# Second attention: scores in plain float32 from one tile of queries and one of key blocks, in place of three passes on high and low parts

## The reference

```
Qp = query @ Wq + bq
K = _l2norm(key @ Wk + bk)
V = value @ Wv + bv
Q = _l2norm(Qp)
... split in 16 heads of 16
scores = einsum('bhqd,bhkd->bhqk', Q, K) * SCALE
attn = softmax(scores)
out = einsum('bhqk,bhkd->bhqd', attn, V)
x = out @ Wo + bo + Qp          # then a layer norm
```

## Time and profile before

| What | Value |
|---|---|
| median of 3 runs | 942.38 us (939.27 to 947.75) |
| the profiled execution | 947.8 us, span 946.0 us |
| mean granted TensorE clock over the span | 0.951 |
| PE busy over the span | 867.4 us (92%) |
| DVE, ACT, POOL busy | 723.1, 527.6, 366.6 us |
| scores of attention 1 (L2112) | 240 matmuls, 50.9 us busy |
| values of attention 1 (L2128) | 640 matmul records, 84.4 us busy |
| query split on DVE (L2330) | 16 operations, 0.657 to 0.692 us each |
| key blocks on POOL (L2549) | 16 operations, 1.37 to 1.40 us each |

### The profile page before, as it was taken

One profiled execution on the slowest core, in us unless ns is written; L12 is line 12 of the kernel. 1 busy time (PEld: TensorE's weight loads), 2 busy tenths in 40 slices (PEclk: granted clock), 3 DMA queues, 4 the chain that ended last, 5 costly groups with the idle time before them and its releaser, 6 DMA issues. The chain is left out here.

```text
span 946.0 us, 18647 instructions
## 1 busy us (share of the span) xinstructions
PE 867.4 (92%) x5904; PEld 793.7 (84%) x5904; DVE 723.1 (76%) x1821; ACT 527.6 (56%) x1454; POOL 366.6 (39%) x412
## 2 busy tenths in 40 slices
PE   5899999999999999999979999996899999999435
PEld 5889999999999988898978999995688888888324
DVE  6788788878878978878656677784525889877888
ACT  4776567656747645546244444443435566664277
POOL 3234333424333426756521211413544757431230
PEclk9999999999999999999999999997768999999758
DMA  9999970000100013434125434434111111000003
GB/s 287 311 336 326 333 229 0 0 0 0 34 0 1 1 34 96 127 108 140 62 85 146 122 110 148 141 124 122 35 50 35 51 40 46 23 1 2 0 22 156
DMA packets 51771, 91.89 MB, mean 97 GB/s; under 512 B 5381, under 2 KB 26298, under 8 KB 51697
## 3 DMA queue, kind: packets, MB, share of 16 engines
q1 hardware_dynamic: 45105, 72.87, 24.0%
q0 software_dynamic: 6592, 18.07, 6.1%
HBM read 34.56 MB, written 56.36 MB: 96 GB/s over the span
## 5 line engine op out<-in xcount | busy, mean ns | idle before, releaser
L535 POOL TENSOR_TENSOR prob<-prob,row_inv 128x462 f32<-128x462 f32 (+1 forms) x96 | 83.8, 875 | 178.8 <-DVE row_inv L711 178.8
L898 PE MATMUL acc<-u,probT 128*128 128x256 f32 (+1 forms) x960 | 134.2, 289 | 1.0 <-DVE u L723 1.0
L595 ACT ACTIVATE prob<-score,neg_max 128x77 f32<-128x77 f32 x512 | 121.2, 353 | 13.3 <-DVE neg_max L705 12.9
L851 PE MATMUL score<-m,xnT 128*128 128x462 f32 (+1 forms) x576 | 122.7, 350 | 0.0
L898 PEld LDWEIGHTS acc<-u,probT 128*128 128x128 f32 (+1 forms) x960 | 119.5, 189 | 1.9 <-DVE u L723 1.4
L851 PEld LDWEIGHTS score<-m,xnT 128*128 128x128 f32 x576 | 96.3, 188 | 5.8
L2128 PEld LDWEIGHTS acc<-vz,prob 128*128 128x128 f32 (+1 forms) x640 | 82.4, 203 | 13.0 <-issue 11.2
L1231 PE MATMUL py<-w1T,hidT 128*128 x426 | 93.0, 354 | 0.0
L585 ACT ACTIVATE probT<-tr 128x512 fp32r<-128x512 f32 (+1 forms) x96 | 52.0, 545 | 66.2 <-PE tr L837 65.8
L1676 POOL DMA_INDIRECT dispatched<-xn,slots x64 | 69.5, 1085 | 43.8 <-DVEq L1460 26.5
L2128 PE MATMUL acc<-vz,prob 128*128 128x34 f32 (+2 forms) x640 | 84.4, 287 | 0.0
(11 more groups left out here) (381 smaller groups left out, 2100.5 us busy)
## 6 DMA issues: line engine op xcount, KB each, us to landing
dispatched<-zeros SPq DMA_DIRECT2D x1, 33664.0 KB, 109.2
xn<-dispatched SPq DMA_DIRECT2D x71, 128.0 KB, 2.0
dispatched<-hid SPq DMA_DIRECT2D x71, 128.0 KB, 1.8
out<-x_res SPq DMA_DIRECT2D x7, 512.0 KB, 2.6
x_res<-in_x SPq DMA_DIRECT2D x1, 3072.0 KB, 15.2
consts<-in_L_ffn_W SPq DMA_DIRECT2D x8, 384.0 KB, 3.5
consts<-in_L_ffn_Ws SPq DMA_DIRECT2D x3, 384.0 KB, 3.6
x_res<-in_x SPq DMA_DIRECT2D x2, 512.0 KB, 10.2
```

The source lines that it names most:

```text
L535: gp.tensor_tensor(pr, pr, row_inv[t % 2][:, heads(k)].unsqueeze(2).to_broadcast([P, BANK_HEADS[k], KEYS]), ALU.mult).then_inc(prob_ready, 1)
L595: last = act.activation(prob[t % 2][:, h * KEYS:(h + 1) * KEYS], score_of(t, k)[:, n * KEYS:(n + 1) * KEYS], ACT.Exp, bias=neg_max[t % 2][ ...
L851: last = pe.matmul(score_of(t, k)[:, 0:BANK_HEADS[k] * KEYS], xnT[blk][i][:, dc, j * P:(j + 1) * P], m[w][:, dc, cols(k)], start=(n == 0 a ...
L898: last = pe.matmul(acc[t % 2][:, 0:D], probT[t % 2][i][0:rows, c, :], u[k][0:rows, c, :], start=(c == 0 and q == 0), stop=(c == KCH - 1 an ...
```

## The change

The high and low tiles go away, for queries and for keys. ACT's copy out of the turned bank becomes the only one, in float32, and its semaphore takes the place of the low part's. POOL builds one `kbd`, in one operation where there were two. The scores of a chunk are one float32 matmul call, started and closed in itself, and the calls of a pair stand one behind the other. Nothing else in any engine's order is moved.

```diff
-    kept = g["consts"][:, KEPT_AT:KEPT_AT + DC * CK].bitcast(F32R).rearrange("p (c k) -> p c k", k=CK)
-    g["k1T"] = [kept, right("k1T_lo", [P, DC, CK], F32R)[:, :, :]]
+    g["k1T"] = g["consts"][:, KEPT_AT:KEPT_AT + DC * CK].rearrange("p (c k) -> p c k", k=CK)
...
-                act.activation(g["k1T"][0][:, f, :], side[:, 0:CK], ACT.Copy).then_inc(s["kT_hi"], 1)
+                act.activation(g["k1T"][:, f, :], side[:, 0:CK], ACT.Copy).then_inc(s["kT_out"], 1)
...
-            if i - 2 in TURN_AT:
-                f = TURN_AT.index(i - 2)
-                dve.wait_ge(s["kT_hi"], f + 1)
-                dve.tensor_tensor(g["k1T"][1][:, f, :], side[:, 0:CK], f32(g["k1T"][0][:, f, :]), ALU.subtract).then_inc(s["kT_lo"], 1)
...
-        kbd = [sb(f"kbd1_{i}", [P, DC, HH, KEYS], F32R) for i in range(2)]
+        kbd = sb("kbd3", [P, DC, HH, KEYS], F32)
...
-        qT = [[sb(f"qT{s}_{i}", [P, DC, TB], F32R) for i in range(2)] for s in range(2)]
+        qT = [sb(f"qT{s}", [P, DC, TB], F32) for s in range(2)]
...
-                pe.wait_ge(s["qT_lo"], DC * n + f + 1)
+                pe.wait_ge(s["qT_out"], DC * n + f + 1)
...
-            for q, (i, k) in enumerate(HI_LO_PASSES):
-                keys = kbd[i][:, f, :, :].rearrange("p h k -> p (h k)")
-                for c in cs:
-                    cc, rows = chunk(c)[1:]
-                    part = query_rows(cc)
-                    last = pe.matmul(score[c % 2][0:rows, :], keys[part, cc * P:cc * P + rows], qT[n % 2][k][part, f, :], start=(q == 0), stop=(q == 2))
-                    if q == 2:
-                        last.then_inc(s["score_mm"], 1)
+            keys = kbd[:, f, :, :].rearrange("p h k -> p (h k)")
+            for c in cs:
+                cc, rows = chunk(c)[1:]
+                part = query_rows(cc)
+                pe.matmul(score[c % 2][0:rows, :], keys[part, cc * P:cc * P + rows], qT[n % 2][part, f, :], start=True, stop=True).then_inc(s["score_mm"], 1)
...
-            act.activation(qT[n % 2][0][:, dc, :], turned(n, 1, dc)[:, :], ACT.Copy).then_inc(s["qT_hi"], 1)
+            act.activation(qT[n % 2][:, dc, :], turned(n, 1, dc)[:, :], ACT.Copy).then_inc(s["qT_out"], 1)
...
-        def dve_split_q(dve, n, dc):
-            hi, lo = qT[n % 2]
-            dve.wait_ge(s["qT_hi"], DC * n + dc + 1)
-            dve.tensor_tensor(lo[:, dc, :], turned(n, 1, dc)[:, :], f32(hi[:, dc, :]), ALU.subtract).then_inc(s["qT_lo"], 1)
...
-            for i in range(2):
-                keys = f32(k1T[i][:, f, batch * KEYS:(batch + 1) * KEYS]).unsqueeze(1).to_broadcast([P, HH, KEYS])
-                last = gp.tensor_tensor(kbd[i][:, f, :, :], keys, g["head_rows"][:, :, :], ALU.mult)
-            last.then_inc(s["kbd_ready"], 1)
+            keys = k1T[:, f, batch * KEYS:(batch + 1) * KEYS].unsqueeze(1).to_broadcast([P, HH, KEYS])
+            gp.tensor_tensor(kbd[:, f, :, :], keys, g["head_rows"][:, :, :], ALU.mult).then_inc(s["kbd_ready"], 1)
```

More of the change, by code:

```diff
@@ L1069, in experts @@
                  "ctx_in", "wk_in", "wv_in", "bias_in", "ctx_mm", "ctx_out", "k_mm", "k_out", "norm_out", "norm_step",
-                 "v_mm", "v_out", "kT_mm", "kT_hi", "kT_lo")
+                 "v_mm", "v_out", "kT_mm", "kT_out")
         s = {n: ctx.enter_context(nc.semaphore(n + "1")) for n in names}
@@ L1276, in pe_turn_keys @@
             else:
-                pe.wait_ge(s["kT_lo"], f)
+                pe.wait_ge(s["kT_out"], f)
             for b in range(B):
@@ L1935, in attention1 @@
         tr, proj = pb("tr3"), pb("proj3")
-        names = ("mv_ready", "eps_done", "rstd_ready", "shift_ready", "xn_ready", "tr_mm", "xT_out", "qT_hi", "qT_lo", "proj_mm", "proj_out", "ssq_done", "root_done",
+        names = ("mv_ready", "eps_done", "rstd_ready", "shift_ready", "xn_ready", "tr_mm", "xT_out", "qT_out", "proj_mm", "proj_out", "ssq_done", "root_done",
                  "qn_ready", "qres_ready", "kbd_ready", "score_mm", "exp_done", "pv_mm",
@@ L2011, in turn_out @@
         def turn_out(n, kind, dc):
-            return s[("xT_out", "qT_lo")[kind]], DC * n + dc + 1
+            return s[("xT_out", "qT_out")[kind]], DC * n + dc + 1
         def pe_transpose(pe, n, kind, dc, src):
@@ L2200, in act_turn_x, with act_turn_q @@
             act.activation(xnT[:, dc, :], turned(n, 0, dc)[:, :], ACT.Copy).then_inc(s["xT_out"], 1)
-        def act_split_q(act, n, dc):
+        def act_turn_q(act, n, dc):
             act.wait_ge(s["tr_mm"], tr_count(n, 1, dc))
-            act.activation(qT[n % 2][0][:, dc, :], turned(n, 1, dc)[:, :], ACT.Copy).then_inc(s["qT_hi"], 1)
+            act.activation(qT[n % 2][:, dc, :], turned(n, 1, dc)[:, :], ACT.Copy).then_inc(s["qT_out"], 1)
         def act_squares(act, n, a):
@@ L2263, in act_first_block @@
             act_exp(act, 0, 9)
-            act_split_q(act, 1, 0)
+            act_turn_q(act, 1, 0)
             act_turned(act, 0, 0)
-            act_split_q(act, 1, 1)
+            act_turn_q(act, 1, 1)
             for a in range(2):
@@ L2294, in act_block @@
             if nxt:
-                act_split_q(act, n + 1, 0)
+                act_turn_q(act, n + 1, 0)
             if nxt2:
@@ L2308, in act_block @@
             if nxt:
-                act_split_q(act, n + 1, 1)
+                act_turn_q(act, n + 1, 1)
         def dve_row_sums(dve):
@@ L2464, in dve_first_block @@
             dve_shift(dve, 2)
-            for dc in range(DC):
-                dve_split_q(dve, 1, dc)
         def dve_block(dve, n):
@@ L2491, in dve_block @@
                 dve_last_stats(dve, n - 2)
-            if nxt:
-                dve_split_q(dve, n + 1, 0)
             dve_residual(dve, n - 1, 1)
@@ L2502, in dve_block @@
             dve_update(dve, n - 1)
-            if nxt:
-                dve_split_q(dve, n + 1, 1)
         def gp_gather(gp, n, first=0, last=TOP_K * TJ):
@@ L2642, in _ @@
                 for dc in range(DC):
-                    act_split_q(act, 0, dc)
+                    act_turn_q(act, 0, dc)
                 act_normalize(act, 1, 0)
@@ L2722, in _ @@
                 dve_value_rows(dve, range(16, len(SPREAD)))
-                for dc in range(DC):
-                    dve_split_q(dve, 0, dc)
                 dve_query_residual(dve, 0)
```

## The result

| | before | changed |
|---|---|---|
| median of 22 runs | 942.24 us | 946.71 us |
| profiled execution, span | 947.8, 946.0 us | 944.79, 943.0 us |
| mean granted clock of the profiled span | 0.951 | 0.959 |

The ratio is 1.0056 (95% interval 1.0035 to 1.0078), 3.3 to 7.3 us. The two profiled executions alone would show the wrong sign, since one execution differs from the next by several microseconds; the ratio rests on all runs. (Two of the changed kernel's executions, of 1125 and 2997 us, were disturbed and are not in the ratio; the median of its other 20 is 945.73.)

The account below looks back on a forecast made before the run. PE was taken to bound the steady blocks. Pairs and singles 21.4, cold rounds 1.9, less 0.7 at the batch change, gave plus 22.6 us; against the median of 942.4 the forecast was 965.0 us, range 950 to 981.

Parts of the forecast that it names:

- What bounds: Steady blocks: PE bounds them, so each microsecond added to PE counts and relief of DVE or POOL is worth nothing.
- The single round: Scores of one chunk: two float32 records, 0.864 us against 0.70, plus 0.165 on each of 15 singles.
- The paired round: Scores of two chunks: matmuls start in program order, three steps, 1.50 us, plus 0.61 on each of 31 pairs.
- rival 2: Paired scores: full overlap of the halves, 1.06 us a pair, plus 7.9 us in all, 950 us; chance 0.11.
- The steady block: Blocks in the middle: from 24.04 to 26.8 us, by four pairs and two singles, PE still busy throughout.
- The cold rounds: Scores of blocks 0 and 1 at 1.2 GHz: the added streaming doubles there, 1.9 us more.
- rival 3: First blocks: the clock stays at 2.4 GHz from 684 us on; with the middle case 950 us; chance 0.08.
- The relief at the change of batch: Block across a batch change: one POOL key operation fewer makes DVE less late, giving at most 0.7 us, taken whole.
- Opening and tail: Start and end of the stage: no gain or loss at the first pair; tail after 875 us of the same length.
- the first pair: Block 0's first scores: 2.8 us at half clock, ending about when ACT's table is loaded; no gain, no loss.
- the two key splits: Key splits at L1322, 0.467 us each: next user 6.5 us later, so removing them is worth nothing.
- rival 4: Not slower: the clock staying up and full overlap of paired scores together, 937 us; chance 0.05.

Follow-up runs that it names:

- e6: Kernel before, with the three float32r passes of a pair's first chunk issued ahead of the second's instead of alternating; ratio 0.9994 to the kernel before.
- e1: Changed kernel with every score matmul over all 128 rows, so a pair's chunks can't use different halves; ratio 1.0146 to the kernel before.
- e11: The changed kernel itself, run again on chip 3 against the kernel before; ratio 1.0027.
- e12: Kernel before with float32 queries, keys and scores in batch 0 alone (blocks 0 and 1), on chip 3; ratio 0.9965 to the kernel before.
- e7: Kernel before with float32 queries, keys and scores in batch 0 alone (blocks 0 and 1), on chip 7; ratio 0.9971 to the kernel before.
- e4: Changed kernel with DVE's 16 query subtractions and POOL's second key operations put back as dead work; ratio 1.0024 to the kernel before.
- e3: Kernel before without query splits and second key operations, all three passes reading the high tiles; ratio 1.0049 to the kernel before.
- e13: Kernel before with float32 queries, keys and scores in batches 1 to 3 alone, on chip 3; ratio 1.0052 to the kernel before.
- e10: Kernel before with float32 queries, keys and scores in batch 0 alone, the scores there over all 128 rows; ratio 0.9967 to the kernel before.
- e9: Kernel before with its float32r scores of batch 0 over all 128 rows; ratio 0.9997 to the kernel before.
- e2: Kernel before with its float32r scores over all 128 rows in all blocks; ratio 1.0033 to the kernel before.

## Why the prediction was wrong, point by point

- **What bounds:** right. PE was busy in all of each steady block, before and after.
- **The single round:** right, 0.86 for the forecast 0.864.
- **The paired round:** wrong, and this is the step that failed. I held that PE starts matmuls in order, so that a pair takes three steps, 1.50. It takes two, 1.06: the bound below, rival 2. e6 shows that order between the halves doesn't matter, e1 that the halves do. My reading, that "the groups in the trace never start out of program order", was of groups, which hide the order of their records; the single records of the kernel before did start out of order, in 16 pairs. 31 x (0.61 - 0.17) = 13.6 us of my 22.6 were this, and 1.1 more in the cold rounds.
- **The steady block:** 25.05, for the 26.8 of the forecast and 24.04 + 4 x 0.17 + 2 x 0.165 = 25.05 of rival 2.
- **The cold rounds:** wrong in sign. I added 1.9 us for longer streams at the low level; the low level itself got shorter. On chip 3 the changed kernel (e11) has a mean clock of 0.954, 89 us at 1.2 GHz, and the kernel before 0.949, 97 us. Across the executions of the kernel before, on each of the three chips, a microsecond less at the low level goes with 0.29 to 0.36 us less time, so the 8 us would be worth 2 to 3. That is rival 3's mechanism, at about a fifth of its size. It is a correlation over whole runs; that the time is saved in the first blocks is borne out by e12 and e7 alone.
- **The relief at the change of batch:** the size right, 0.7; the reason wrong, since e4 has it with the queries' and key blocks' work back on DVE and POOL. In the changed kernel DVE was busy for 13.6 us less and POOL for 13.7, for the forecast 10.9 and 11.1.
- **Opening and tail:** right, nothing. But the first pair ran at the full clock in the profiled execution, where I had said half, and took 1.11 us in place of 2.8. What the two key splits were worth no run shows by itself.
- **The sum as it came out:** 31 x 0.17 + 15 x 0.165 - 0.7 = 7.0, cold part 0.8, clock minus 2 to 3: plus 4.8 to 5.8, against a measured 3.3 to 7.3. Rival 2 with a small part of rival 3; I had given the two together, rival 4, a chance of 0.05. The agreement is no proof of the last term: e3 has some 2.6 us that nothing here explains.

## What to carry to other kernels

Price packed matmuls on separate row halves by the longer half plus a fixed 0.4 us for going in and out (0.20 in the round and 0.19 in the group behind it, at the full clock here), whatever their order in the queue. Before a forecast rests on a rule of order, look for single records that could break it, by a form that tells them apart: a group's line hides them. Where the granted clock falls in a stretch, a change there is not priced by its streaming alone: try it in that stretch and in the rest separately, as e12 and e13 do here with opposite signs.

## What the runs showed of the hardware

- A matmul on one row half starts past older ones that wait for the other half: in e6 the second chunk's first call, fourth in the program, starts with the first, and the pair stays at 0.89 us.
- Float32 matmuls on different row halves run side by side: 1.06 us for two calls of 512 columns, against 1.72 for the same two on whole rows.
- A round on halves costs about 0.2 us beyond its streaming, and the group behind it 0.19 more: 1.90 against 1.71 for 16 records of values.
- The granted clock, as a mean of the run, is higher with float32 scores in the first blocks: 0.958 (e4), 0.957 (e7), and 0.954 and 0.957 (e11, e12), where the kernel before had 0.954, 0.951 and 0.949; 0.963 with float32 on whole rows (e10) against 0.949. Why is open, and float32r on whole rows gave 0.955 (e9) and 0.960 (e2) against 0.951 with the same first two blocks.
